# Gate steps of the next chunk one pair earlier in an eight-expert mixture layer, on one Trainium2 core

## The reference

```
t = t + ffn(_ln_t(t))                     # 8*4096 tokens of 64 channels
router_probs = softmax(x @ router_w + router_b)          # 8 experts
top_p, top_i = top_k(router_probs, 2)
top_p = top_p / sum(top_p)
expert_out = einsum("bnd,edc->bnec", x, expert_w) + expert_b
out = sum over the two chosen experts of top_p * expert_out
```

## Time and profile before

| | us |
|---|---|
| median of 3 runs | 964.58 (963.37 to 965.38) |
| profiled execution, its own time | 966.94 |
| span of its instructions | 965.1 |
| TensorE matmul busy | 854.9 (89%) |
| VectorE busy | 774.8 (80%) |
| GpSimd busy | 568.8 (59%) |
| ScalarE busy | 506.2 (52%) |

### The profile page before, as it was taken

The page is one execution under the profiler, slowest core; times in us unless marked ns, Lnnn a source line. Parts: engine busy times, 40 slices in busy tenths (PEclk is TensorE's granted clock), DMA queues, the critical chain, the costliest instruction groups (busy, mean ns, idle before and its releaser), DMA issues.

```text
span 965.1 us, 24392 instructions
## 1 busy us (share of the span) xinstructions
PE 854.9 (89%) x9482; PEld 701.7 (73%) x9482; DVE 774.8 (80%) x1421; ACT 506.2 (52%) x1051; POOL 568.8 (59%) x504
## 2 busy tenths in 40 slices
PE   6996788677999999996899999999568999999998
PEld 6986777645676666654899999999536666667665
DVE  5767698878899999999787677765788899997884
ACT  2477385786666666311344444343278566676411
POOL 3770203157788887796654334420226788888888
PEclk9996577878999999999899999999859999999999
DMA  9988100103677777673787877787000010101101
GB/s 378 346 286 260 49 1 2 40 14 155 271 304 288 293 291 294 275 314 126 263 281 258 283 269 254 259 282 261 1 1 23 23 45 23 44 27 41 45 35 53
DMA packets 48291, 163.09 MB, mean 169 GB/s; under 512 B 9424, under 2 KB 9936, under 8 KB 46032
## 3 DMA queue, kind: packets, MB, share of 16 engines
q1 hardware_dynamic: 48208, 161.96, 46.3%
HBM read 93.46 MB, written 68.49 MB: 168 GB/s over the span
## 4 chain that ended last, share of the span: by engine, by line
PE 55%; DVE 24%; POOL 6%; issue 6%; ACT 5%; DMA 3%; SPq 1%; POOLq 0%; DVEq 0%; ACTq 0%
PE pair L1692 24%; DVE R L904 7%; PE pair L1619 7%; PE pair L1605 5%; PE pair L1606 5%; PE pair L1616 4%; DMA X<-x_rows 3%; PE pair L1492 3%; POOL R L571 3%; ACT pair L1249 2%; DVE R L660 2%; DVE R L833 2%; DVE R L844 2%; PE pair L1583 2%; DVE work L660 2%
## 5 line engine op out<-in xcount | busy, mean ns | idle before, releaser
L904 DVE TENSOR_TENSOR R<-pair,R 128x896 f32<-128x896 f32 x256 | 275.3, 1083 | 50.8 <-PE pair L1606 50.0
L571 POOL TENSOR_TENSOR R<-R 128x768 f32<-128x768 f32 x128 | 231.9, 1811 | 94.4 <-DVE R L904 78.4
L1692 PE MATMUL pair<-R 128*128 (+4 forms) x2880 | 227.6, 243 | 9.2 <-DVE R L982 9.2
L1692 PEld LDWEIGHTS pair<-R 128*128 128x128 f16 x2880 | 224.9, 98 | 12.1 <-issue 9.5
L1249 ACT ACTIVATE pair<-X,work 128x64 f32<-128x64 f32 x480 | 166.6, 394 | 124.1 <-DVE R L844 121.6
L1605 PE MATMUL pair<-work,R 128*128 128x448 f16 x512 | 185.8, 363 | 24.7 <-DVE R L904 24.5
L1606 PE MATMUL pair<-work,R 128*128 128x448 f16 x512 | 184.9, 361 | 0.0
L581 POOL TENSOR_TENSOR R<-R 128x512 f32<-128x512 f32 x128 | 164.7, 1286 | 10.0
L997 DVE COPY R<-R 128x1152 f32<-128x1152 f32 x64 | 92.7, 1449 | 65.3 <-PE pair L1692 64.6
L1367 ACT COPY R<-R 128x1152 f32<-128x1152 f32 x64 | 82.0, 1282 | 117.3 <-PE pair L1692 117.3
L1619 PE MATMUL pair<-R,ident_sb 128*128 128x256 f32 x496 | 130.3, 386 | 0.0
(11 more groups left out here) (137 smaller groups left out, 1292.8 us busy)
## 6 DMA issues: line engine op xcount, KB each, us to landing
taps_halves<-R SPq DMA_DIRECT2D x128, 458.5 KB, 3.3
R<-taps_halves SPq DMA_DIRECT2D x64, 917.0 KB, 4.7
X<-x_tok SPq DMA_DIRECT2D x4, 2048.0 KB, 18.1
out<-X SPq DMA_DIRECT2D x15, 512.0 KB, 2.6
R<-spec_pairs SPq DMA_DIRECT2D x16, 272.0 KB, 5.3
X<-x_rows SPq DMA_DIRECT2D x4, 1024.0 KB, 11.0
R<-x_chan SPq DMA_DIRECT2D x4, 1024.0 KB, 14.0
X<-x_rows SPq DMA_DIRECT2D x2, 2048.0 KB, 27.2
```

Of the source, the lines that this page charges most:

```text
L571: pool.tensor_tensor(pr[:, :, 192:384], pr[:, :, 0:192], pr[:, :, 192:384], ALU.add).then_inc(half_ready, 1)
L904: dve.tensor_tensor(pr.rearrange("p t (e c) -> p t e c", c=C), pair[p % 2][:, :].rearrange("p (t e c) -> p t e c", t=2, c=C)[:, :, 0:NE - ...
L1692: mm = pe.matmul(acc[:, y0:y1, x0:x1, :], blocks[i % 2][:, ks, 2 - y, 1 - x, :], src[:, y0 + y:y1 + y, x0 + x:x1 + x, :], start=(ks == 0 a ...
```

## The change

```diff
-        GATES_AT = {8: (0, 1), 9: (2, 3), 10: (4, 5), 11: (6, 7), 12: (8, 9), 13: (10, 11), 14: (12, 13, 14)}
+        GATES_AT = {7: (0, 1), 8: (2, 3), 9: (4, 5), 10: (6, 7), 11: (8, 9), 12: (10, 11), 13: (12, 13, 14)}
         PARTS_AT = (0, 1, 1, 3, 3, 4, 5, 7)
-        EXP_AT, ROOT_AT = 12, 11
+        EXP_AT, ROOT_AT = 11, 10
```

## The result

The changed kernel took 956.03 us in the median of 4 runs (955.77 to 958.52), the kernel before 964.98 (963.37 to 965.80, 4 runs) beside it: ratio 0.9908, 95% interval 0.9891 to 0.9925. A second series gave 958.52 (956.50 to 958.97) against 965.19, ratio 0.9931 (0.9905 to 0.9956). So it is 6.7 to 9.0 us faster, where I forecast 5.84. The direction held, the first time lies 0.8 us under my range. The profiled execution took 955.84 us, its span is 954.1.

What follows compares the result with a forecast made beforehand. VectorE (pairs 8 to 15) and TensorE (pair 1 to pair 8) were taken to set the pace by turns in each chunk. Gains of 4.16 + 0.13 + 0.79 + 0.76 = 5.84 us off 964.58 gave 958.7 us, range 956.8 to 962.0.

Steps and rivals of the forecast that it cites:

- (a): VectorE, steady chunk: steps 0 and 1 go before pair 8, which starts 0.27 us late; idle time hides 0.52 of 0.79.
- (b): VectorE, pair 8 to pair 15: two steps fewer remain, 13.31 us instead of 14.10, so pair 15 starts 0.52 earlier.
- (c): TensorE's pair 1 of the next chunk follows `weigh_pair` 15 as before and can take the whole 0.52 us.
- (d): TensorE's pair 13 starts 0.27 us late; the sum of pair 14 absorbs it, as ScalarE's copy starts 0.20 earlier.
- (e): VectorE's pair 14, behind steps 12 to 14, starts 0.63 us late; 0.2 remains before TensorE's pair 0, the tightest place.
- (f): GpSimd's last quad comes 0.79 us late against the rest; 0.9 stay before the sum needing it, so no cost.
- (g): The seed of the root keeps its place in ScalarE's list: no effect.
- TensorE is the bound: Rival: TensorE has the most work and its idle time would come back elsewhere; nothing changes, 964.6 us, chance 0.08.
- more than that: Rival: each steady chunk gains 0.79 us, with pair 8 late for another reason or steps slipped in wholly; 956.6, chance 0.04.
- Sum: Whole kernel: 4.16 + 0.13 + 0.79 + 0.76 = 5.84 us gained, giving 958.7 us, 0.6% faster.
- How the numbers follow: Whole kernel: own sum given 0.70, 957.5 to 960.3 around it; range 956.8 to 962.0, faster by over 0.2% 0.87.

Runs made afterwards that it cites:

- after_stats5: The changed kernel with the statistics of pair 7 moved to pair 5; 956.46 us, ratio 0.9903 to the kernel before.
- two_steps: The kernel before with only gate steps 0 and 1 moved from pair 8 to pair 7; 964.29 us, ratio 0.9994.
- gates_only: The kernel before with all gate steps one pair earlier, exponential and seed of the root left in place; 957.77 us, ratio 0.9924.
- stats5_late6: after_stats5 with gate steps and exponential back at the old pairs in chunk 6 of layer 0 alone; 958.13 us, ratio 0.9922 to the kernel before.
- before_late12: The kernel before with twelve extra VectorE statistics instructions (results unused) in the opening of layer 1's mixture; 965.26 us, ratio 1.0000.
- after_late6: The changed kernel with six extra VectorE statistics instructions (results unused) in the opening of layer 1's mixture; 959.48 us, ratio 0.9937 to the kernel before.
- exp_only: The kernel before with only the exponential and the seed of the root one pair earlier, gate steps left; 981.37 us, ratio 1.0165.

## Why the prediction was right in its direction and too small

The steps in the order of the prediction, each against the changed kernel's trace.

(a) Right. Pair 8 stands 3.78 us behind pair 6 instead of 3.53: 0.25 late, 0.27 forecast. after_stats5 shows that the statistics ahead of it are the cause.

(b) Right. Pair 15 is at 17.08 behind pair 6 instead of 17.63, 0.55 earlier, 0.52 forecast. two_steps adds a condition that I had not stated: without steps 2 to 14 closing up, VectorE waits for TensorE's pair 10 and the gain is 0.04.

(c) Right. Pair 1 starts at 18.22 instead of 18.76, 1.14 us behind `weigh_pair` 15 as before (1.13). TensorE's idle time ahead of it fell from 0.65 to 0.15.

(d) Half right. The copy on ScalarE came 0.23 earlier (11.21 instead of 11.44; 0.20 forecast), and without the exponential's move the sum of pair 14 is 0.25 late. That this would reach the end of the chunk was my implied conclusion, and gates_only refutes it: I let TensorE's earlier work last 0.17 us beyond the start of its last matmul, while the next one starts 0.03 us after it (356.65 and 356.68). Where the exponential moves alone, on the other hand, it costs 1.18 a chunk.

(e) Right. In a steady chunk pair 14 is 0.60 late (15.48 instead of 14.88; 0.63 forecast) and TensorE's pair 0 starts at 351.89 without a wait.

(f), (g) No loss in the eight chunks: each is shorter by the 0.54 that VectorE gained, so neither GpSimd nor the seed of the root took anything.

Chunk 6 of layer 0, where I put 0, lost 0.31. I had argued that steps which change places inside an unbroken queue cost nothing. But pairs 8 to 13 move inside it. Nothing hides the two steps ahead of pair 8 here, so pair 13 is 0.79 late instead of 0.27, and TensorE's pair 15, which needs its buffer, waits:

```profile
411.68 0.36 PE L1605 MATMUL pair<-work,R 128*128 128x448 f16 x1 [0.37 <-DVE R L904]
...
413.98 0.35 PE L1605 MATMUL pair<-work,R 128*128 128x448 f16 x1
...
414.55 0.35 PE L1606 MATMUL pair<-work,R 128*128 128x448 f16 x1
```

TensorE's pair 0 of chunk 7 (413.98) comes 0.5 late behind it, and VectorE's pair 0, which was 0.2 from having to wait, starts at 414.99 after idle time. The profile names no releaser for it, but the last matmul of TensorE's pair 0 starts at 414.55 and takes 0.35:

```profile
414.99 1.09 DVE L904 TENSOR_TENSOR R<-pair,R 128x896 f32<-128x896 f32 x1 [0.22 <-issue]
```

stats5_late6 shows by taking it back that the order in chunk 6 is the cause. Its expectation names the wrong pair: TensorE's pair 15 waited for pair 13, not pair 0 for pair 14.

Chunk 5 of layer 0 gained 0.18 (0.13 forecast), chunks 5 and 6 of layer 1 gained 0.89 and 0.80 (0.79 and 0.76). At chunk 5 of layer 1, profiles with the same work there differ by 0.1 as well (before_late12 gains 0.10 on before, after_late6 loses 0.10 on the changed kernel). Together: 4.38 + 0.18 - 0.31 + 0.89 + 0.80 = 5.94 us, against a sum of 5.84. No rival came true by its mechanism: "TensorE is the bound" fails by the 0.54 in each of eight chunks, and "more than that" gives the time but not its cause, since pair 8 is late.

**The step that failed** is the "Sum", and with it the range in "How the numbers follow". Every term takes the durations of its rows as fixed, and so do the rivals from which the lower bound of 956.8 comes: a term for TensorE's clock was put at nothing, without a reason. A low-clock stretch of 3.4 us lay in the profile before, at 754.2, and the changed kernel does not have it; that is worth 1.66 us. With it the change gives 5.94 + 1.66 = 7.6 us, 7.65 with the small terms. That lies inside both measured intervals (0.9891 to 0.9925 of 964.98 is 7.2 to 10.5 us; 0.9905 to 0.9956 of 965.19 is 4.2 to 9.2). before_late12 and after_late12 show that a delay of VectorE ahead of layer 1 can remove such a stretch and bring one back. Why exactly one distance has it and the next not stays open.

This term alone would not have put the time under my range: 964.58 - 7.65 is 956.9, just inside. The last 0.9 us come from which executions the first series drew. 955.77, 955.84, 956.22 and 956.50 us have a granted clock of 0.936 over the whole kernel, 958.41, 958.52, 958.63 and 958.97 have 0.934. The first series has three of the first group, the second series one. The two profiles are one of each, and they are 2.6 us apart already where the mixture of layer 0 begins, with nothing changed ahead of it. The median of all eight is 957.5 and that of the 41 executions of before that ran beside the experiments 965.3: 7.8 us, near the 7.65 of the traces. What makes an execution fall into one group or the other stays open. So the 5.84 I forecast for the schedule was near, with the loss of chunk 6 made up for by small gains elsewhere, which is luck; the direction and the steady chunks were not.

## What to carry to other kernels

Where two engines take turns in setting the pace, work moved into the waiting engine's idle time pays only if what follows it closes up in the half that this engine sets; moving the first steps alone gave nothing. A dependent step on a third engine, here the exponential, may move together with its producer; moved ahead of it, it cost 1.18 us a chunk. And before a sum of fractions of a microsecond is called the forecast, list the stretches of low granted clock in the profile before: each that lies behind the change and follows a pause of TensorE can vanish or appear through a mere shift, for 1.2 to 2.9 us here, as much as the change itself won in two to five chunks. And compare two versions in their traces, from the first changed instruction on: four executions can lie by 2.5 us to one side because of what happens ahead of it.

## What the runs showed of the hardware that I had not expected

A pause of TensorE of 1.46 or 1.47 us, the same nine times in exp_only, met half the clock (0.50) in two cases and full clock in seven. A pause of 2.20 us met it in five of twelve profiles, and a tenth of a microsecond in the distance above divides those with it from those without. One kernel keeps its side: both profiles of before have that stretch, neither of the changed kernel. A version that is 0.30 us better in its own steps (stats5_late6) lost 1.22 us to such a stretch. A delay of 2.15 us of VectorE's work cost only 0.5 in the trace, as a low-clock stretch of 3.4 us went away with it (before_late12, ratio 1.0000). The eight executions of the changed kernel lie in two groups 1.9 us apart, with granted clocks of 0.936 and 0.934.
